# Grouping the scratch fills between GpSimd's gathers: two fills of 128x1024 per tile in place of eight of 128x256

## The reference, cut to what matters

```
# block 0: deformable convolution in a residual bottleneck
h   = relu(bn1(conv1x1(x, w1)))                 # 128 -> 32 channels
off = conv3x3(h, woff) + boff                   # 27 channels: 9 taps x (dy, dx), 9 masks
samp = bilinear(h, base + off) * sigmoid(mask)  # 9 taps per pixel, four corners each, zero outside
h   = relu(bn2(einsum(samp, w2) + dcn_b))       # 32 channels
x   = relu(bn3(conv1x1(h, w3)) + x)             # 128 channels
# block 1: attention over all 3136 pixels of an image
f, g, h = wf x + bf, wg x + bg, wh x + bh       # 16 channels each
attn = softmax(f^T g)                           # 3136 x 3136 per image
out = gamma * (wv (h attn^T) + bv) + x
```

## Time and profile before

| | us |
|---|---|
| median of 3 runs | 1559.62 |
| lowest and highest run | 1557.89, 1575.72 |
| profiled execution, device time | 1568.37 |
| its span, first to last instruction | 1566.6 |
| first gather starts | 43.5 |
| last gather starts | 1403.9 |

### The profile page before, as it was taken

How to read it: one execution, slowest core, us unless ns; L and a number is a source line. 1 busy time by engine, 2 the same in 40 slices (tenths; PEclk the granted TensorE clock), 3 DMA queues, 4 the chain that set the end, 5 groups by cost and what they waited for, 6 DMA issues and landing times.

```text
span 1566.6 us, 18944 instructions
## 1 busy us (share of the span) xinstructions
PE 1190.6 (76%) x5781; PEld 507.6 (32%) x5781; DVE 968.9 (62%) x2171; ACT 681.5 (43%) x1400; POOL 1215.9 (78%) x1673
## 2 busy tenths in 40 slices
PE   5617356388887877898588697898767877889997
PEld 2213122133433333343233242443223323333342
DVE  5444153387866764788466576767655865568781
ACT  2103022143654443465354444546344544457765
POOL 3788888888888888888888888888888888870000
PEclk9756758575978777688777776959577987799998
DMA  3231322211111111121111111121111111110000
GB/s 144 73 120 53 102 75 66 82 42 46 38 42 43 44 50 47 56 66 44 42 43 45 44 50 56 53 58 41 45 40 44 43 50 55 55 51 1 1 12 30
DMA packets 37325, 82.10 MB, mean 52 GB/s; under 512 B 15322, under 2 KB 17486, under 8 KB 36712
## 3 DMA queue, kind: packets, MB, share of 16 engines
q0 software_dynamic: 28224, 57.86, 13.5%
q1 hardware_dynamic: 8964, 22.93, 4.0%
q10 hardware_dynamic: 36, 0.10, 0.0%
HBM read 66.23 MB, written 14.59 MB: 52 GB/s over the span
## 4 chain that ended last, share of the span: by engine, by line
POOL 69%; PE 14%; issue 11%; DVE 5%; DMA 1%; another core or an unknown queue 0%; ACT 0%; POOLq 0%; DVEq 0%
POOL G L477 54%; POOL pad L484 15%; PE PV L633 3%; DVE mxp L1060 2%; PE L1a L602 1%; PE L1b L602 1%; PE L1c L652 1%; PE L1c L669 1%; PE L2a L619 1%; PE L2b L619 1%; DVE fold L1190 1%; DVE G L1038 0%; PE T L586 0%; PE L1c L662 0%
## 5 line engine op out<-in xcount | busy, mean ns | idle before, releaser
L477 POOL DMA_INDIRECT G<-table,IDX x882 | 946.6, 1073 | 187.9 <-issue 158.8
L1060 DVE TENSOR_REDUCE mxp<-L1b 112x1 f32<-112x448 f32 x378 | 234.3, 620 | 143.8 <-PE L1b L602 65.0
L812 ACT ACTIVATE H<-L2b 112x448 f32<-112x448 f32 x370 | 200.5, 542 | 280.1 <-PE L2b L619 187.0
L1060 DVE TENSOR_REDUCE mxp<-L1a 112x1 f32<-112x448 f32 x379 | 234.4, 618 | 69.8 <-PE L1a L602 32.5
L812 ACT ACTIVATE H<-L2a 112x448 f32<-112x448 f32 x370 | 200.1, 541 | 135.0 <-PE L2a L619 93.4
L484 POOL MEMSET pad<- 128x256 f32 x784 | 257.4, 328 | 0.5
L602 PE MATMUL L1b<-G,F 96*112 96x448 bf16 x378 | 174.0, 460 | 88.0 <-DVE mxp L1060 50.6
L633 PE MATMUL PV<-H,HT 112*17 112x448 f32 x1568 | 232.1, 671 | 0.9 <-ACT H L812 0.9
L602 PE MATMUL L1a<-G,F 96*112 96x448 bf16 x379 | 172.1, 454 | 68.9 <-DVE mxp L1060 54.7
L1038 DVE TENSOR_TENSOR G<-G,CW 128x640 f32<-128x640 f32 x196 | 145.8, 750 | 98.2 <-DMA G<-table,IDX 98.2
L619 PE MATMUL L2b<-F,G 99*112 99x448 bf16 x370 | 157.9, 427 | 2.4 <-issue 2.0
(11 more groups left out here) (124 smaller groups left out, 1314.3 us busy)
## 6 DMA issues: line engine op xcount, KB each, us to landing
G<-table,IDX POOLq DMA_INDIRECT x882
table<-TS SPq DMA_DIRECT2D x24, 256.0 KB
out<-X SPq DMA_DIRECT2D x11, 448.0 KB
X<-xt SPq DMA_DIRECT2D x3, 1568.0 KB, 9.7
out<-X SPq DMA_DIRECT2D x6, 224.0 KB
offd<-OFS SPq DMA_DIRECT2D x28, 47.2 KB
OFG<-offd SPq DMA_DIRECT2D x13, 94.5 KB
X<-xt SPq DMA_DIRECT2D x1, 1120.0 KB, 6.5
```

Of the source, the lines that this page charges most:

```text
L477: eng.indirect_dma_start(G[:, j, k * 4 * CB:(k + 1) * 4 * CB], None, table[0:images * POS, :], bass.IndirectOffsetOnAxis(ap=IDX[:, g % IRI ...
L812: nc.scalar.activation(E[:, y % ERING, :], l2(y)[0:KT, 0:CHUNK], ACT.Exp).then_inc(s_exp, 1)
L1060: eng.tensor_reduce(mxp[:, p.q, qt, kc:kc + 1], l1(x)[0:KT, 0:CHUNK], AX.X, ALU.max)\
```

## The change

After it, GpSimd fills `pad` only behind the third and the sixth gather of a tile (k = 2 and k = 5), and `pad` has 1024 columns in place of 256. All gathers, their order, their semaphores and all other engines' programs stay as they are. The wait count of `s_pad` is renumbered to the two fills of a tile.

```
+BURST = 3
...
-        pad = sb("pad", [128, 256])
+        pad = sb("pad", [128, 1024])
...
-                        if k < TAPS - 1:
-                            after(eng, s_pad, (TPG * g + j) * (TAPS - 1) + k)
+                        if k % BURST == BURST - 1 and k < TAPS - 1:
+                            after(eng, s_pad, 2 * (TPG * g + j) + k // BURST)
                             eng.memset(pad[:, :], 0.0).then_inc(s_pad, 1)
```

## The result

Four runs of the changed kernel took 1537.99 to 1551.77 us, median 1542.05; the kernel before, with one run more than the three above, 1557.89 to 1575.72 us, median 1562.32. The ratio is 0.989, 95% interval 0.984 to 0.993: about 1.1% faster. The prediction was 1572 us (range 1540 to 1660), 0.8% slower. The time lies in the range and within the 2% that was given the most chance, but a slowdown was forecast and a speed-up came: the sign was wrong.

What follows compares the result with a forecast made beforehand. GpSimd's program of gathers and fills was taken as the bound; 4.09 us added less 3.94 us removed per tile, +0.144 us, gave +12.7 us over 88 tiles: 1559.6 + 12.7 = 1572 us, range 1540 to 1660.

Steps and rivals of the forecast that it cites:

- GpSimd's program is the bound: From 43.5 us to the last gather GpSimd never waits for another engine; the end moves as its 88th tile moves.
- The run lengths, the direct pair, the fill, the gap behind it: GpSimd's gathers in runs of three and six; direct gap 0.305 us, long fill 0.964, gap behind 0.165; sum +0.144 us per tile.
- The stretching of gathers: Gathers' 109 us above plain duration, where VectorE runs two-input instructions; taken as unchanged, 0 with 8 us to either side.
- L: Follow-up theory, not in the prediction: a long fill during VectorE's tile work takes up instructions that would otherwise hold a gather.
- The sign of being wrong: The prediction was to be wrong if GpSimd's time per tile differed by more than 0.35 us from 14.0.
- Which lines move the end: Line 1038's last multiply waiting for gathers was the 88th tile's, so +0.144 us per tile counted over 88 tiles: +12.7 us.
- Rival A: GpSimd's long runs dearer than pairs: third and later gathers cost 0.185 us more each, 81 us, 1653 us; chance 0.36.
- B: Gap between direct gathers shrinks within a run to 0.165 us, -74 us, giving 1498 us; chance 0.14.
- C: VectorE's two-input instructions shut out while gathers run: 2.3 us later per tile, up to 225 us, 1797 us; chance 0.04.
- D: No effect: TensorE would have held up the 22 waited-for tiles anyway; the end stays at 1560 us; chance 0.04.
- A premise of B: VectorE's 98.2 us of waits at line 1038 could give back what shorter gaps between gathers save.
- S: Follow-up theory, not in the prediction: VectorE holds a gather right behind a gather less than one behind a fill.

Runs made afterwards that it cites:

- nofill: The changed kernel with no fills of `pad` at all, so all 882 gathers form one run; 1391.5 us, ratio 0.893 to the kernel before.
- small3: The changed kernel with its two fills per tile at 256 columns in place of 1024; 1432.7 us, ratio 0.921 to the kernel before.
- thin_before: The kernel before with VectorE's four two-input instructions per tile cut to about 32 columns; ratio 0.945 to the kernel before.
- shift_before: The kernel before with 16 columns filled behind k = 0 and 496 behind k = 5, so gather k = 1 starts earlier; ratio 0.991 to the kernel before.
- shift_after: The changed kernel with a 256-column fill added behind k = 0 and 797 columns behind k = 2, so k = 1 starts later; ratio 0.992 to the kernel before.
- before_again: The kernel before run once more, unchanged, for a second profile; ratio 1.0002 to the kernel before.
- thin_after: The changed kernel with VectorE's four two-input instructions per tile cut to about 32 columns; 1473.7 us.

## Why the prediction was wrong

**GpSimd's program is the bound.** Right, and more strictly than I used it. Its length from first to last gather and the time move together: nofill -174 us and about -168 us (1391.5 against 1559.0), small3 -127 and -126, thin_before -92 and -86, the change -17.5 and -20 us.

**The run lengths, the direct pair, the fill, the gap behind it.** Right, each within 0.01 us; the sum of these terms is +15.6 us for 98 tiles, predicted 14.1.

**The stretching of gathers.** This step failed: "VectorE issues the same instructions after the change ... I take 0, with 8 us to either side." It measured -32.8 us on the mean of three profiles each, and that outweighed the +15.6 us. I had counted how much of GpSimd's time is open to VectorE, as if the two met at random. They don't: in 22 to 52 tiles VectorE waits for the very gathers that GpSimd issues, so its first multiply has a fixed delay to GpSimd's next gathers. The earlier trace rows held it: the multiply at 1269.18, 1.51 us after the end of the ninth gather; the next tile's k = 1 starts 0.30 + 0.95 + 0.33 + 0.17 = 1.75 us after that end before, and 0.30 + 0.95 + 0.30 = 1.55 us after the change. At k = 1 the stretch fell by 27.1 - 5.6 = 21.5 us, and shift_before and shift_after show that this part follows where the fills stand. How much of the 32.8 us the phase explains is open: moved alone, k = 1 changed the whole stretch by 10 and by 3 us. The other 11 us (87.9 - 76.6 outside k = 1) are in profiles that overlap; L would fit them, but isn't shown.

**The sign of being wrong.** The prediction was to be wrong if GpSimd's time per tile differed by more than 0.35 us from 14.0. It was 1342.6 / 98 = 13.7 us, 0.30 off, so this sign stayed silent: 0.35 us is more than twice the 0.144 us that the change was held to cost. The last gather's start showed it: 1384.8 us, where 1418 was named. Two figures of the working are slightly off and bear on nothing: the immune share before is 33.2%, not 33.4%, and A's upper bound is 8.9 x 88 = 783 us, not over 800.

**Which lines move the end.** The choice of the 88th tile was one execution's: the last waited-for tile was the 98th in before_again and the 95th in the changed kernel's first profile; it changes the 88 in the sum to at most 98, 1.4 us.

**Rival A** (0.36) fell: gathers third or later in a run take 0.94 to 0.95 us, in the change and in nofill. **B** fell: the gap is 0.30 us within runs, also in nofill. Faster came by a way that no rival held. **C** fell: in nofill 63 tiles' first multiplies began inside a running gather, and they took 0.82 us at the median and 0.85 at most. By the exclusive lock that the prediction cites from the Trainium skill (SBUF — State Buffer, SBUF: two separate sides) a gather that started first would have kept them out; here the trace disagrees, with these durations. **D** fell with small3 and nofill.

**A premise of B.** I took the 98.2 us of waits at line 1038 as what a faster GpSimd could give back. nofill gave back 168 us and still shows waits of 102.5 us at that line; the same kernel before showed 205.6 us in before_again. The sum of a wait in one profile is neither stable nor a cap. Why the later stages kept pace wasn't taken apart; TensorE's busy time fell from 1190.6 to 1138.1 us at a granted clock of 0.782 in place of 0.767.

## What to carry to other kernels

When one engine waits for what another issues, their next meeting has a nearly fixed phase: here 517 of 532 waited-for first multiplies began 1.44 to 1.75 us after the ninth gather's end. So before calling a contention term unchanged, line up one waited-for case of the rows by start and end and ask which instruction starts first after the edit. Moving 0.2 us of fill from one place in the tile to another made the kernel before 0.9% faster, almost as much as the change; the reverse move in the changed kernel cost next to nothing, so such a gain has to be measured. And price the whole of an idle-looking instruction on the engine that bounds the kernel: here leaving out the scratch fills was worth 10.7%, regrouping them 1.1%.

## What the runs showed of the hardware

**When a gather is held.** Over the fourteen profiles of unthinned kernels, for gathers met by one two-input VectorE instruction alone: where the instruction was on at least 0.1 us before the gather's start and lasted until 0.25 us after it or longer, all 240 gathers were held, and they ended 0.82 us after the instruction's end, behind a fill (135) and behind a gather (105) alike, so S falls. Where the instruction began within 0.4 us after the gather's start, about a third of 739 were held; but of the 90 among them that were first multiplies begun after a wait, none. Where it began later, about one in twenty. So a gather can be held by what runs near its start, and not over its whole 0.95 us. Why the waited-for multiplies differ from the others isn't shown.

**A long fill holds VectorE.** In the changed kernel's rows above, the cast of line 1077, on 112x4 elements, runs from 1252.80 to 1254.09 and ends with the fill (1253.09 to 1254.06). The three small one-input groups, before, after the change, and in nofill (busy us, mean ns):

```profile
L1072 DVE TENSOR_SCALAR NM<-mx 112x4 f32<-112x4 f32 x54 | 12.5, 232 | 0.0
L1080 DVE CAST MS<-res 112x4 bf16<-112x4 f32 x54 | 12.5, 231 | 1.1
L1076 DVE CAST MS<-NM 112x4 bf16<-112x4 f32 x54 | 11.7, 216 | 1.0
```

```profile
L1073 DVE TENSOR_SCALAR NM<-mx 112x4 f32<-112x4 f32 x54 | 18.5, 342 | 0.0
L1081 DVE CAST MS<-res 112x4 bf16<-112x4 f32 x54 | 17.6, 326 | 1.1
L1077 DVE CAST MS<-NM 112x4 bf16<-112x4 f32 x54 | 15.0, 278 | 1.1
```

```profile
L1072 DVE CAST MS<-NM 112x4 bf16<-112x4 f32 x54 | 11.1, 206 | 1.0
L1076 DVE CAST MS<-res 112x4 bf16<-112x4 f32 x54 | 10.5, 194 | 1.1
L1068 DVE TENSOR_SCALAR NM<-mx 112x4 f32<-112x4 f32 x54 | 10.4, 193 | 0.0
```

Together 36.7, 51.1 and 32.0 us: these three groups cost VectorE 14 us more after the change. The two-input TENSOR_TENSOR groups of the same 112x4 size between them (lines 1078 and 1082) took 154 and 155 ns before and 152 and 155 after, so the fills don't hold those. What the 14 us cost the kernel wasn't tested; VectorE has 4% of its chain.

**One kernel, two clocks, two bounds.** thin_after took 1473.7 us on one chip, with a granted clock of 0.768 and a chain that is 70% GpSimd and 9% TensorE in its profile, and 1556.3 us on another, with 0.727, 22% GpSimd and 52% TensorE. The unthinned kernel before took 1559.0 and 1564.3 us on these chips, with clocks of 0.73 to 0.76 on both. Why the thinned kernels got less clock on the second chip isn't known.
